# A mixture-of-experts kernel on one core: two of the shared expert's tiles moved behind the routed tiles

## The reference, cut to what matters

```python
def expert_ffn(x, wg, wu, wd):
    h = jax.nn.silu(x @ wg) * (x @ wu) / SCALING
    return h @ wd
def moe(x, ...):
    shared = expert_ffn(x, sh_gate, sh_up, sh_down)
    scores, idx = jax.lax.top_k(jax.nn.sigmoid(x @ router_w + router_b), 2)
    w = ...  # scores over their sum, spread over the 7 experts
    for e in range(7):
        combined = combined + w[..., e:e + 1] * expert_ffn(x, r_gate[e], r_up[e], r_down[e])
    return shared + combined
...
out = h + moe(rmsnorm(h, ln2_w), ...)
```

## Time and profile before

| | us |
|---|---|
| median of 3 runs | 1253.35 |
| the profiled execution | 1256.78 |
| span of its trace, first to last instruction | 1255.0 |
| TensorE busy | 1145.3 (91%) |
| VectorE busy | 728.1 (58%) |
| ScalarE busy | 572.9 (46%) |
| GpSimd busy | 333.9 (27%) |
| chain that ended last, by engine | TensorE 73%, DMA 8%, VectorE 7%, SyncE's queue 4% |
| mean granted TensorE clock | 0.96 |

### The profile page before, as it was taken

How to read it: one execution, slowest core, us unless ns; L and a number is a source line. 1 busy time by engine, 2 the same in 40 slices (tenths; PEclk the granted TensorE clock), 3 DMA queues, 4 the chain that set the end, 5 groups by cost and what they waited for, 6 DMA issues and landing times.

```text
span 1255.0 us, 18112 instructions
## 1 busy us (share of the span) xinstructions
PE 1145.3 (91%) x5687; PEld 798.4 (64%) x5687; DVE 728.1 (58%) x1714; ACT 572.9 (46%) x1248; POOL 333.9 (27%) x275
## 2 busy tenths in 40 slices
PE   5989989999999899999989899989989999999960
PEld 5755545665666456557657667755657888888850
DVE  6465486468545865656646766574545764444433
ACT  3324365445544565555455555544456743222310
POOL 0413133201320231002022202200235644555530
PEclk9969999999999899999989999998999999999985
DMA  7153344336322742553584473486567735656569
GB/s 262 34 168 118 98 145 130 90 98 202 120 64 89 228 131 64 184 168 105 175 229 140 144 247 95 144 250 162 145 215 249 250 126 106 109 111 116 106 147 328
DMA packets 105609, 191.10 MB, mean 152 GB/s; under 512 B 24140, under 2 KB 34796, under 8 KB 103980
## 3 DMA queue, kind: packets, MB, share of 16 engines
q1 hardware_dynamic: 96700, 169.61, 43.7%
q0 software_dynamic: 8512, 19.93, 8.9%
q10 hardware_dynamic: 304, 0.40, 0.1%
HBM read 118.98 MB, written 65.53 MB: 147 GB/s over the span
## 4 chain that ended last, share of the span: by engine, by line
PE 73%; DMA 8%; DVE 7%; SPq 4%; issue 3%; ACT 3%; POOL 1%; DVEq 0%; ACTq 0%; POOLq 0%
PE psum L976 12%; PE psum L793 9%; PE psum L794 8%; PE psum L795 8%; PE psum L939 6%; PE psum L960 6%; PE psum L1054 4%; PE psum L1056 4%; PE psum L1055 4%; PE psum L802 3%; PE psum L1081 2%; SPq L554 2%; PE psum L1083 2%; PE psum L1082 2%; PE psum L1023 2%
## 5 line engine op out<-in xcount | busy, mean ns | idle before, releaser
L1298 ACT ACTIVATE probs<-psum 128x512 f32<-128x512 f32 (+3 forms) x512 | 257.4, 517 | 217.2 <-PE psum L963 108.9
L1722 DVE TENSOR_REDUCE nmax<-psum 128x1 f32<-128x512 f32 x256 | 171.3, 686 | 124.2 <-PE psum L939 119.4
L939 PE MATMUL psum<-stack 96*128 96x512 f32 (+3 forms) x512 | 211.0, 417 | 10.1 <-DVE nmax L1725 6.7
L976 PE MATMUL psum<-probs,vals 128*33 128x512 f32 (+3 forms) x1024 | 212.3, 537 | 0.0
L960 PE MATMUL psum<-stack 97*128 97x512 f32 (+3 forms) x512 | 199.7, 391 | 11.8 <-ACT probs L1298 6.2
L1725 DVE CUSTOM_DVE_ANT_0 psum<-psum,causal 128x128 f32<-128x128 f32 (+3 forms) x256 | 123.8, 503 | 74.6 <-PE psum L939 73.6
L939 PEld LDWEIGHTS psum<-stack 96*128 96x128 f32 x512 | 100.5, 196 | 83.2 <-issue 58.4
L960 PEld LDWEIGHTS psum<-stack 97*128 97x128 f32 x512 | 99.7, 195 | 38.8 <-ACT probs L1298 16.7
L1433 POOL TENSOR_TENSOR o_lo<-o_chunk,o_hi 128x512 fp32r<-128x512 f32 x31 | 42.0, 1354 | 276.4 <-ACT o_hi L1140 276.4
L976 PEld LDWEIGHTS psum<-probs,vals 128*33 128x33 f32 x1024 | 50.0, 112 | 101.5 <-issue 76.4
L793 PE MATMUL psum<-w_hi,xh 128*128 128x512 f32 (+1 forms) x256 | 96.8, 378 | 5.2 <-POOL xl L1401 3.6
(11 more groups left out here) (245 smaller groups left out, 2283.1 us busy)
## 6 DMA issues: line engine op xcount, KB each, us to landing
stack<-split_s SPq DMA_DIRECT2D x378, 128.0 KB, 3.3
split_s<-split SPq DMA_DIRECT2D x64, 512.0 KB, 3.9
inverse_sums<-inverse_s SPq DMA_DIRECT2D x31, 256.0 KB
xt<-in_x_dram SPq DMA_DIRECT2D x4, 1024.0 KB, 5.3
x_s<-yt SPq DMA_DIRECT2D x4, 1024.0 KB, 5.6
xt<-x_s SPq DMA_DIRECT2D x4, 1024.0 KB, 5.3
res<-x_s SPq DMA_DIRECT2D x4, 1024.0 KB, 10.3
yt<-in_x_dram SPq DMA_DIRECT2D x4, 1024.0 KB, 6.0
```

What stands on the lines that cost most here:

```text
L939: sq.filled(nc.tensor.matmul(psum[:, sq.bank(M), 0:n], st[:, 0, t * P:(t + 1) * P], st[:, 1, 0:n], start=True, stop=True), M)
L976: nc.tensor.matmul(psum[at_:at_ + VW, o.bank(p), lo:S], vals[k % 2][:, t, head_of(q, side), :], probs[:, M % NX, lo:S], start=(t == 0), st ...
L1298: sk.cleared(nc.scalar.activation(probs[:, M % NX, lo:S], psum[:, sk.bank(M), lo:S], ACT.Exp, scale=SCALE), M)
L1722: sq.cleared(V.tensor_reduce(out, psum[:, sq.bank(M), :], AX.X, ALU.max, negate=True), M)
```

## The change

Shared tiles 14 and 15 no longer run in front of the routed tiles but behind them, as tiles 52 and 53 (`LATE`); the routed tiles become 14 to 51. Loads of rows for the late tiles go to SyncE behind its stores. The results of the late tiles stay on chip (`late_tile_y`), and VectorE adds them to batch 3 of `second_sums` before the final sums. Their rows in `acc2_s` are zeroed at the start, by two more DMAs. `second_sums` and `first_sums` move up in SBUF behind the shared expert's weights, and all four loads of `second_sums` now wait until the routed tiles are through TensorE. The router's work is drawn together: `find_slots` follows `weigh_and_place` in slot 5, slots 6 to 9 make two chunks each, the products run in slots 7 to 10, the tables are read at slot 10, and expert 0 is split two slots earlier. The products and all other work of a tile are unchanged.

```diff
@@ -246,11 +246,23 @@
 DIVIDED = [(k, c) for k in range(NB) for c in range(NC) if not by_turns(k, 2 * c)]
 NV = len(VALUE_NO)
 
-NSHARED = B * NT
+NLATE = 2
+NSHARED = B * NT - NLATE
 NROUTED = (2 * B * S - NR) // P + NR
-NTILES = NSHARED + NROUTED
-ROUTED = range(NSHARED, NTILES)
+NTILES = B * NT + NROUTED
+ROUTED = range(NSHARED, NSHARED + NROUTED)
+LATE = range(ROUTED.stop, NTILES)
 SPARE = P
+
+
+def rows_at(i):
+
+    return (i if i < NSHARED else i - NROUTED) * P
+
+
+def rows_loads(i):
+
+    return 16 * (sum(n % 2 == i % 2 for n in range(i + 1) if n not in ROUTED))
 
 
 def to_second(r):
@@ -432,8 +444,10 @@
         upto, tok1 = work("upto", [P, P]), work("token_plus_1", [P, B * NT])
         ef, rf, rtmp = work("expert_f", [P, NROUTED]), work("row_f", [P, NROUTED]), work("row_tmp", [P, NROUTED])
         assert work.where <= last_.where - ew_size * (2 * NR - 1)
-        final = Strip(WEIGHTS_AT)
+        final = Strip(WEIGHTS_AT + 2 * ew_size)
         sum2, sum1 = final("second_sums", [P, B, NT, D]), final("first_sums", [P, B, NT, D])
+        late_y = final("late_tile_y", [P, NLATE, D])
+        assert final.where <= last_.where
 
         v_ld, v2_ld = sem("vectors_loaded"), sem("small_tables_loaded")
         c_ok, r_ok, m_ok = sem("constants_ready"), sem("rounded_constants_ready"), sem("vals_and_stack_set")
@@ -482,16 +496,16 @@
         routed, out_st = sem("slots_ready"), sem("output_stored")
         experts_known = sem("expert_of_tile_ready")
         sum2_ld, sum_ld = sem("second_sums_loaded"), [sem(f"sums_loaded{b}") for b in range(B)]
-        summed = sem("sums_added")
+        late_ok, summed = sem("late_tiles_added"), sem("sums_added")
 
         XB, GB, HB, YB = (4, 5), (2, 3), 6, 7
-        X2_SLOT, ROUTER_SLOT, CHOOSE_SLOT, COUNT_SLOT, READ_SLOT = 1, 2, 3, 5, 12
+        X2_SLOT, ROUTER_SLOT, CHOOSE_SLOT, COUNT_SLOT, READ_SLOT = 1, 2, 3, 5, 10
         STEP_CONST, STEP_FIRST, STEP_COUNTED, STEP_PLACED, STEP_SLOTS, STEP_CHUNK = 11, 20, 30, 42, 48, 3
         HI_EARLY = {0: ((1, 0), (1, 1)), 1: ((3, 0),), 2: ((3, 1),), 3: ((3, 2),), 4: ((2, 0),), 5: ((2, 2),), 6: ((4, 1),),
-                    7: ((5, 0),), 8: ((5, 2),), 9: ((6, 1),), 13: ((0, 1),)}
+                    7: ((5, 0),), 8: ((5, 2),), 9: ((6, 1),), 11: ((0, 1),)}
         HI_LATE = {0: ((1, 2),), 4: ((2, 1),), 5: ((4, 0),), 6: ((4, 2),), 7: ((5, 1),), 8: ((6, 0),), 9: ((6, 2),),
-                   12: ((0, 0),), 13: ((0, 2),)}
-        TABLE_MID, TABLE_LATE = {8: (0,), 9: (2,), 10: (3,), 11: (5,), 12: (6, 7)}, {8: (1,), 10: (4,)}
+                   10: ((0, 0),), 11: ((0, 2),)}
+        TABLE_MID, TABLE_LATE = {7: (0,), 8: (2,), 9: (4,), 10: (6, 7)}, {7: (1,), 8: (3,), 9: (5,)}
         CHUNKS = 2 * B
         side = psum[:, 0, :]
         hit = side[:, 0:NT * NROUTED].rearrange("p (j n) -> p j n", n=NROUTED)
@@ -627,7 +641,7 @@
             def load_rows(i):
                 if i >= 2:
                     sp.wait_ge(t_mm, i - 1)
-                sp.dma_start(xg[:, i % 2, :], x2_s[i * P:(i + 1) * P, :]).then_inc(xg_ld[i % 2], 16)
+                sp.dma_start(xg[:, i % 2, :], x2_s[rows_at(i):rows_at(i) + P, :]).then_inc(xg_ld[i % 2], 16)
 
             def store_acc(i):
                 sp.wait_ge(acc_ok, NT * (i - B + 1))
@@ -657,6 +671,8 @@
             sp.wait_ge(c_ok, CONSTANTS)
             for t_ in (acc_s, acc2_s, x2_s):
                 sp.dma_start(t_[B * S:, :], oh[:, 0, :].bitcast(F32)).then_inc(spare_set, 16)
+            for i in LATE:
+                sp.dma_start(acc2_s[rows_at(i):rows_at(i) + P, :], oh[:, 0, :].bitcast(F32)).then_inc(spare_set, 16)
 
             load_x(1)
             store_k(0, 0)
@@ -765,13 +781,13 @@
                 if s == 8:
                     load_expert(0)
 
+            for i in LATE:
+                load_rows(i)
             last2 = max(r for r in range(NROUTED) if to_second(r))
             sp.wait_ge(y_added[1], 16 * (last2 // 2 + 1))
-            sp.wait_ge(y_mm, NSHARED)
-            for b in range(B - 1):
+            sp.wait_ge(y_mm, ROUTED.stop)
+            for b in range(B):
                 sp.dma_start(sum2[:, b], by_batch(acc2_s)[b]).then_inc(sum2_ld, 16)
-            sp.wait_ge(y_mm, NTILES)
-            sp.dma_start(sum2[:, B - 1], by_batch(acc2_s)[B - 1]).then_inc(sum2_ld, 16)
             for q in range(2):
                 sp.wait_ge(y_added[q], 16 * (NROUTED // 2))
             for b in range(B):
@@ -1014,7 +1030,7 @@
                 if i in ROUTED:
                     pe.wait_ge(xg_got[i % 2], 16 * (ROUTED.index(i) // 2 + 1))
                 else:
-                    pe.wait_ge(xg_ld[i % 2], 16 * (i // 2 + 1))
+                    pe.wait_ge(xg_ld[i % 2], rows_loads(i))
                 if i >= 2:
                     pe.wait_ge(x_lo, i - 1)
                 else:
@@ -1216,7 +1232,7 @@
                 elif kind == "o_split":
                     c, = at_
                     if j == 0 and c == 0:
-                        act.wait_ge(spare_set, 3 * 16)
+                        act.wait_ge(spare_set, (3 + NLATE) * 16)
                     if j and c == 0:
                         ring.wait_full(act, ("out", j - 1, NT - 1))
                     act.wait_ge(o_div, NC * j + c + 1)
@@ -1342,9 +1358,10 @@
             def shared_out(i):
                 q = i % 2
                 act.wait_ge(y_mm, i + 1)
-                if i >= 2:
+                if 2 <= i < NSHARED:
                     act.wait_ge(y_st[q], 16 * (i // 2))
-                nc.scalar.activation(yb[:, q, :], psum[:, YB, :], ACT.Copy, scale=1.0 / SCALING).then_inc(y_out, 1)
+                to = late_y[:, LATE.index(i), :] if i in LATE else yb[:, q, :]
+                nc.scalar.activation(to, psum[:, YB, :], ACT.Copy, scale=1.0 / SCALING).then_inc(y_out, 1)
 
             hi_of_x(0)
             hi_of_x(1)
@@ -1366,7 +1383,7 @@
                     beside(("x2", LAST, 3))
                 for e, c in HI_EARLY.get(s, ()):
                     split_expert(e, c)
-                if s < NSHARED:
+                if s not in ROUTED:
                     shared_out(s)
                 if s == CHOOSE_SLOT - 1:
                     act.wait_ge(lg_ok, B)
@@ -1955,29 +1972,12 @@
                     choose_second()
                 if s == COUNT_SLOT:
                     weigh_and_place()
-                if s == COUNT_SLOT + 1:
+                if s == COUNT_SLOT:
                     find_slots()
-                    chunk_tiles(0)
-                if s == COUNT_SLOT + 2:
-                    chunk_rows(0)
-                    chunk_tiles(1)
-                    chunk_rows(1)
-                if s == COUNT_SLOT + 3:
-                    chunk_tiles(2)
-                    chunk_rows(2)
-                    chunk_tiles(3)
-                if s == COUNT_SLOT + 4:
-                    chunk_rows(3)
-                    chunk_tiles(4)
-                    chunk_rows(4)
-                if s == COUNT_SLOT + 5:
-                    chunk_tiles(5)
-                    chunk_rows(5)
-                    chunk_tiles(6)
-                if s == COUNT_SLOT + 6:
-                    chunk_rows(6)
-                    chunk_tiles(7)
-                    chunk_rows(7)
+                if COUNT_SLOT < s <= COUNT_SLOT + CHUNKS // 2:
+                    for n in range(2 * (s - COUNT_SLOT - 1), 2 * (s - COUNT_SLOT)):
+                        chunk_tiles(n)
+                        chunk_rows(n)
                 if s == READ_SLOT:
                     read_tables()
                     read_weights()
@@ -1987,6 +1987,11 @@
                     split_expert(0, 2)
 
             dve.wait_ge(sum2_ld, 16 * B)
+            dve.wait_ge(y_out, NTILES)
+            for i in LATE:
+                at_ = sum2[:, B - 1, rows_at(i) // P % NT, :]
+                V.tensor_tensor(at_, at_, late_y[:, LATE.index(i), :], ALU.add).then_inc(late_ok, 1)
+            dve.wait_ge(late_ok, NLATE)
             for b in range(B):
                 dve.wait_ge(sum_ld[b], 16)
                 for t in range(NT):
```

## The result

The changed kernel takes 1244.37 us (median of 6 runs, 1242.54 to 1248.08) against 1255.84 us for the kernel before in 6 runs: ratio 0.9918, 95% interval [0.9897, 0.9939], so by this ratio 10.3 us less (7.7 to 12.9); the two medians themselves are 11.5 us apart. A later series of 6 runs gave 0.9931 [0.991, 0.9951], which is 8.6 us less (6.1 to 11.3). The forecast was 10.5 us.

The account below looks back on a forecast made before the run. TensorE, busy throughout the routed tiles, delays a closing row of transfers by whatever precedes those tiles. 8.5 us from the routed stage plus 2.0 from the tail make 10.5: median 1253.35 to 1242.9 us, range 1240.5 to 1248.5.

Parts of the forecast that it names:

- both terms: Routed stage starts 8.5 us sooner (9.54 less waits of 0.6 and 0.4); the closing transfers give 2.0 us more.
- Slot 6: find_slots moved ahead of tile 6's low part of h: TensorE waits 0.5 us, the start behind it 0.6.
- Slots 7 to 9: Two chunks and two products per slot of 5.67 us: TensorE waits for nothing, 1.2 us over.
- Slot 10: Product 7 wants its chunk 0.45 us into the slot, ready at 0.86: a wait of 0.4 us.
- Gather, expert 0, start: First gather issued near 1012.9, bound 0.6 us but taken as 0; expert 0's transfer and two starting DMAs cost nothing.
- The tail: Closing scatters, loads and stores: last scatters 4.8 and 9.25 us, first sums' loads 2.3 sooner; gain 2.0, bounds -2.6 to +4.0.
- the hole of the earlier trace: DMA engines moved only 58 GB/s from 1230.5 to 1233; this was to absorb the second sums' loads ending some 2 us later.
- The lower bound of the tail, -2.6: No hole is filled; all ends as much later as the last load of the second sums starts.
- No change: Rival: the end is tied to the late tiles or their loads, time stays at 1253.4 us; chance 0.06.
- TensorE held in every slot: Rival: the router's links hold TensorE in each of slots 7 to 10, 1.4 us each; 1248.1 us; chance 0.14.
- That the tail gives back: Rival: second sums' loads start later and nothing makes up for it, 8.5 - 2.6 = 5.9, so 1247.5 us; chance 0.12.
- The slower one: Rival: late first gather at tile 14's turn, 5 us wait and halved clock cost 14 us; 1256.9 us; chance 0.04.

Follow-up runs that it names:

- the kernel with GpSimd busy: Kernel before, with GpSimd's last expert piece held to run beside two links of VectorE's table reading; end 282.14 us behind shared tile 4's low part of h, 3.0 later.

## Why the prediction was right

**Direction and mechanism** came as forecast for the routed stage: the routed tiles set the start of the tail, TensorE is busy through them, and two tiles moved behind them are two slots won. **The size** is nearer than the sum deserves: 10.5 us predicted, 10.3 measured, but behind the anchor both terms were smaller, 7.7 for 8.5 and 1.4 for 2.0, 9.1 in all. That 10.3 stands so close to 10.5 is luck: its interval reaches from 7.7 to 12.9, and the later series gave 8.6.

**Slot 6:** 0.6 us forecast; the turn behind it is 0.71 us later than before (14.50 for 13.79 from the anchor). **Slots 7 to 9:** 5.67 us each and no wait, as worked out. **Slot 10:** 0.4 forecast; the slot took 5.93 us against 5.69 for slot 12 before, so 0.24.

**Slot 11** was missed. The prediction gave the reading of the tables the same 4.2 us as before and saw GpSimd's end only as what the first gather waits for. The changed kernel runs the link beside a GpSimd piece, where GpSimd had been idle before (for 5.49 us up to the gather), and loses 0.83 us: that slot takes 6.29 us for 5.46. With all that the shift is 9.54 - 0.71 - 0.24 - 0.83 = 7.76, measured 7.72, and not 8.5. The Trainium skill's rule of the shared port pair (SBUF — State Buffer, Who interferes with whom) bears on this link, and the prediction did not weigh it.

**Gather, expert 0, start:** the gather was issued 37.3 us behind the anchor (forecast 37.0), behind the late link and not behind GpSimd's piece itself, and its tile turned 6.4 us later without a wait. The start's two DMAs fit the gap, as SyncE's queue of the changed kernel shows:

```profile
23.48 1.72 SPq L675 DMA_DIRECT2D acc_s<-o_hi  x2
32.26 0.38 SPq L616 DMA_DIRECT2D xt<-in_x_dram  x1
```

**The tail** went transfer by transfer as worked out: the last but one scatter took 4.84 us (4.8), the last 8.90 (9.25), and the loads of the first sums went out 2.7 us sooner than the shift alone gives (2.3). VectorE's two adds took 1.29 us, and it then still waited 1.49 us for the first sums, so they cost nothing. What was mis-sized is what this is worth at the end, 1.4 us for 2.0. The prediction carried the 2.3 us of the first sums' loads nearly whole to the end, and let the hole of the earlier trace rows take up the later start of the second sums. The hole was filled, and then there was none left: from 1209 to 1239 the busy share of the DMA engines is 0.98 or more in every 3 us (384 GB/s in the row above), and the end is set by the stream of 12 MB (8 of loads, 4 of stores) behind the first load. It follows the start of that stream, and not the first sums' loads. The wait for the last down product stood in the prediction on both sides, as what lets the scatter land in 4.8 us and as a late start to be absorbed; it did not say that this wait is the whole gain of the tail and needs no late tile: alone it gives 3.2 us. Its last part, which the late tiles add, is a loss of 1.8, and 3.2 - 1.8 is the 1.4 measured. The lower bound of the tail, -2.6, has no row behind it; the fourth load of the second sums was issued at 1215.59, and 1218.1 less that is 2.5.

**The rivals.** No change is excluded by the intervals; ScalarE is done with the last late tile at 1213.5, and VectorE starts on the first sums 10 us later. TensorE held in every slot is excluded by the turns of slots 7 to 9. That the tail gives back is excluded by three profiles in which it gave 1.0 to 1.6 us. The slower one needed a wait of TensorE of 5 us; behind the anchor there was none above 1.23. But it asked for too long a wait: in the kernel with GpSimd busy, 2.41 us were enough for the clock to fall, though for some 3 us and not 17. What a wait of 5 us costs there was not run.

## What to carry to other kernels

When a transfer that adds to memory shares the DMA engines with a burst of loads, look for the order that lets the short one, for which others wait, finish first; here starting a 4 MB burst 1.2 us later took 3 us off the end. When a packed schedule slides an instruction under another engine's work, check what both operands lie in, not only how long it took when that engine was idle. Where runs scatter by more than an edit gives, count from a point that both kernels reach by the same work, and still hold the result against the time of the whole kernel: a gain behind such a point can be lost ahead of it.

## What the runs showed that I had not expected

A VectorE instruction on 38 columns can take 1.03, 1.73 or 2.24 us in place of 0.18, each time to the end of the GpSimd instruction beside it, and 0.20 us with its source in PSUM. The last but one scatter with add takes 4.5 to 5.0 us when the loads are issued 1.7 us behind it or later, and 9.2 us when they are issued within half a microsecond; nothing was measured between. And the attention part in front of all this, the same in every kernel but for two small DMAs, varied by 7.5 us from profile to profile.
